# Norm of batch 0's FFN output moved into the last FFN, operands kept in DRAM; 57 instead of 51 FFN units in batch 1's first pass

## What is computed

```
x = x + layernorm(attn(layernorm(x)))     # projections, conv, heads' coefficients,
                                          # a recurrence over the 2048 tokens, group norm, gate, out_W
x = x + layernorm(ffn(layernorm(x)))      # router: mean over tokens -> 2 of 8 experts, softmax weights
# ffn: y_k = gelu(x @ W1[k] + b1[k]) @ W2[k] + b2[k];  out = w_0 y_0 + w_1 y_1   (k: the two chosen experts)
```

## Time and profile before

| | |
|---|---|
| median of 3 runs | 1680.47 us (1678.22 to 1681.45) |
| profiled execution | 1677.81 us, span 1675.6 us |
| TensorE matmul busy | 1248.9 us (75%) |
| VectorE busy | 1267.0 us (76%) |
| ScalarE busy | 409.7 us (24%) |
| GpSimd busy | 68.0 us (4%) |
| mean granted clock of TensorE | 0.879 |
| DMA | 94.34 MB, 56 GB/s over the span |

### The profile page before, as it was taken

One profiled execution on the slowest core, in us unless ns is written; L12 is line 12 of the kernel. 1 busy time (PEld: TensorE's weight loads), 2 busy tenths in 40 slices (PEclk: granted clock), 3 DMA queues, 4 the chain that ended last, 5 costly groups with the idle time before them and its releaser, 6 DMA issues. The chain is left out here.

```text
span 1675.6 us, 12210 instructions
## 1 busy us (share of the span) xinstructions
PE 1248.9 (75%) x4124; PEld 736.0 (44%) x4124; DVE 1267.0 (76%) x1885; ACT 409.7 (24%) x628; POOL 68.0 (4%) x32
## 2 busy tenths in 40 slices
PE   3970554513688888589699999396888786899997
PEld 1440222202344445345465555263544454566665
DVE  4769999998999985758789999987999957100111
ACT  2431000000002015343532232132010143323332
POOL 0000012110000000000001211100000000000000
PEclk9995767656799999779899999698999997999999
DMA  4000100003011120210023222214111010222221
GB/s 151 1 7 0 50 38 38 38 0 126 13 50 38 38 100 6 104 54 7 26 76 101 88 88 76 75 39 176 50 38 39 11 51 1 82 76 78 73 76 75
DMA packets 51676, 94.34 MB, mean 56 GB/s; under 512 B 4640, under 2 KB 39840, under 8 KB 50720
## 3 DMA queue, kind: packets, MB, share of 16 engines
q1 hardware_dynamic: 51616, 93.58, 16.0%
HBM read 73.64 MB, written 19.92 MB: 56 GB/s over the span
## 5 line engine op out<-in xcount | busy, mean ns | idle before, releaser
L486 PE MATMUL ps<-wshare,uT 128*128 128x512 f32 x512 | 244.3, 633 | 55.7 <-DVE kz L1261 55.7
L593 PE MATMUL ps<-kz 128*128 128x256 f32 x1024 | 245.2, 383 | 20.0 <-ACT kz L786 15.4
L579 PE MATMUL ps<-kz 128*128 128x512 f32 x512 | 243.3, 598 | 3.5 <-DMA kz<-in_w 3.3
L593 PEld LDWEIGHTS ps<-kz 128*128 128x128 f32 x1024 | 196.0, 192 | 103.6 <-issue 64.0
L486 PEld LDWEIGHTS ps<-wshare,uT 128*128 128x128 f32 x512 | 101.4, 204 | 178.8 <-issue 117.7
L428 PE MATMUL ps<-wshare,xnT 128*128 128x512 f32 x256 | 146.2, 724 | 35.2 <-ACT ps L661 35.2
L786 ACT ACTIVATE kz<-ps,small 128x512 f32<-128x512 f32 x128 | 87.4, 685 | 296.0 <-PE ps L579 295.8
L1419 DVE TENSOR_TENSOR kz<-ps,b_s 128x256 f32<-128x256 f32 x16 | 6.3, 413 | 180.7 <-PE ps L593 180.7
L579 PEld LDWEIGHTS ps<-kz 128*128 128x128 f32 x512 | 98.3, 193 | 80.6 <-issue 74.6
L420 PE MATMUL ps<-ident,uT 128*128 128x128 f32 x256 | 44.0, 302 | 113.4 <-DVE work L1139 79.1
L721 ACT ACTIVATE kz<-ps 128x512 f32<-128x512 f32 x32 | 19.1, 597 | 371.4 <-PE ps L471 371.4
(11 more groups left out here) (250 smaller groups left out, 1793.4 us busy)
## 6 DMA issues: line engine op xcount, KB each, us to landing
kz<-in_w SPq DMA_DIRECT2D x128, 256.0 KB, 2.9
kap_d<-kz SPq DMA_DIRECT2D x26, 512.0 KB, 2.7
kz<-kap_d SPq DMA_DIRECT2D x26, 512.0 KB, 3.2
uT<-in_x SPq DMA_DIRECT2D x8, 512.0 KB, 5.9
wshare<-in_wq SPq DMA_DIRECT2D x2, 2048.0 KB, 7.8
kz<-in_x SPq DMA_DIRECT2D x2, 2048.0 KB, 12.9
coef<-in_x SPq DMA_DIRECT2D x2, 2048.0 KB, 7.7
wshare<-in_wk SPq DMA_DIRECT2D x2, 1024.0 KB, 11.1
```

The source lines that it names most:

```text
L486: t = mm(ps[:, 2 * (j % 2) + c, :], uT3[:, k, j * P:(j + 1) * P], wq_s[:, k, c, :], start=(k == 0), stop=(k == KI - 1))
L579: t = mm(ps[:, 4 + i % 2, :], w1_r[r][:, k, (f % 2) * P:(f % 2 + 1) * P], x2T[:, k, n * 512:(n + 1) * 512], start=(k == 0), stop=(k == KM ...
L593: t = mm(ps[:, 6 + q // 2, (q % 2) * DM:(q % 2 + 1) * DM], hbuf(i)[:, q * P:(q + 1) * P], w2_r[r][:, f % 2, :], start=(f == 0 and q % 2 == ...
```

## The change

`expert_norm` is gone. After batch 0's FFN its output is stored in DRAM (`f_d`), and the combined bias too (`b2_d`, one row); VectorE does only the two bias instructions (`output_bias`) between `chunk_scan` and `pass_2`. In the last FFN SyncE loads f, bias and x1 into `uT` and `xnT`, which are free then, and `first_norm` does batch 0's norm on VectorE ahead of batch 1's first block; the scaling is on VectorE instead of ScalarE. ScalarE's square root for it (`first_root`) stands behind unit 8. The output of batch 0 is stored behind weight pair 13. In `UNITS` the last entry is 57, so that six of the 13 units behind `turn_ends` lie in the last step of pass 1. The kernel's work is otherwise the same.

```diff
-UNITS = [15] + [15 + 12 * i // 5 for i in range(L)]
+UNITS = [15] + [15 + 12 * i // 5 for i in range(L - 1)] + [57]
...
+        f_d = nc.dram_tensor("f_d", (P, L, DM), F32).ap()
+        b2_d = nc.dram_tensor("b2_d", (1, DM), F32).ap()
...
-        x1_back = kz[:, 5120:9216].rearrange("p (j d) -> p j d", j=L)
...
+        f_back, x1_back, b2_back = x_in, x_c, xnT[:, 0, 0:DM]
...
                 if b > 0:
                     load_pairs(b - 1, chosen, pairs_for(UNITS[L]), NF // 2)
-                    sp.wait_ge(h_ready, b * NF)
-                    sp.wait_ge(x1_stored, 16 * b)
-                    sp.dma_start(x1_back, x1_d[:]).then_inc(x1_loaded, 16)
-                    sp.wait_ge(d_done, b * NF)
+                    sp.wait_ge(b2_ready, b)
+                    sp.dma_start(b2_d[:], b2_s[0:1, 0]).then_inc(b2_stored, 16)
+                    sp.wait_ge(f_used, b * NCH)
+                    sp.dma_start(f_d[:], r_tok).then_inc(f_stored, 16)
                 for j in range(3, L):
                     if b > 0 and j == 5:
-                        sp.wait_ge(out_ready, b)
-                        sp.dma_start(out[b - 1].rearrange("(c j) d -> c j d", j=L), x1_back).then_inc(out_stored, 16)
+                        sp.wait_ge(f_stored, 16 * b)
...
-            load_pairs(B - 1, chosen, 0, NF // 2)
+            load_pairs(B - 1, chosen, 0, WR)
+            sp.wait_ge(f_stored, 16)
+            sp.dma_start(f_back, f_d[:]).then_inc(f_loaded, 16)
+            sp.wait_ge(b2_stored, 16)
+            sp.dma_start(b2_back, b2_d.to_broadcast([P, DM])).then_inc(b2_loaded, 16)
+            sp.wait_ge(x1_stored, 16)
+            sp.dma_start(x1_back, x1_d[:]).then_inc(x1_loaded, 16)
+            load_pairs(B - 1, chosen, WR, 14)
+            sp.wait_ge(out_ready, 1)
+            sp.dma_start(out[0].rearrange("(c j) d -> c j d", j=L), x1_back).then_inc(out_stored, 16)
+            load_pairs(B - 1, chosen, 14, NF // 2)
...
                 if b > 0:
                     experts(b - 1, UNITS[L], NF)
-                    last_root(b - 1)
-                    act.wait_ge(out_stored, 16 * b)
...
+                    if i == 8 and b == B - 1:
+                        first_root()
                     if f == 3 and n > 0 and b == B - 1:
                         block_root(n - 1)
...
-            def last_root(b):
-                act.wait_ge(fin_vec, b + 1)
+            def first_root():
+                act.wait_ge(fin_vec, 1)
                 af(t1, mv[:, :, 1], ACT.Sqrt, bias=eps5).then_inc(fin_act, 1)
-                act.wait_ge(fin_ln, b + 1)
-                for j in range(L):
-                    af(r_tok[:, j], r_tok[:, j], ACT.Identity, scale=rs2[:, j:j + 1], bias=nb[:, j:j + 1]
-                       ).then_inc(fn_ready, 1)
...
+            def first_norm():
+                dve.wait_ge(f_loaded, 16)
+                dve.wait_ge(b2_loaded, 16)
                 for j in range(L):
-                    dve.wait_ge(f_used, b * NCH + j // 4 + 1)
-                    t = mark(tt(r_tok[:, j], r_tok[:, j], b2c, ADD))
+                    t = mark(tt(f_back[:, j], f_back[:, j], b2_back, ADD))
                     if j > 0:
                         after(t - (2 if j > 1 else 1))
-                        stats(j - 1, r_tok[:, j - 1])
+                        stats(j - 1, f_back[:, j - 1])
                 after(t)
-                moments(stats(L - 1, r_tok[:, L - 1])).then_inc(fin_vec, 1)
+                moments(stats(L - 1, f_back[:, L - 1])).then_inc(fin_vec, 1)
+                dve.wait_ge(fin_vec, 1)
+                dve.wait_ge(fin_act, 1)
                 link(v.reciprocal(rs2, t1))
+                link(stt(nb, mv[:, :, 0], -1.0, rs2, MUL, MUL))
+                dve.wait_ge(x1_loaded, 16)
+                for j in range(L + 1):
+                    if j < L:
+                        t = mark(tsc(f_back[:, j], f_back[:, j], rs2[:, j:j + 1], nb[:, j:j + 1], MUL, ADD))
+                    if j > 0:
+                        after(t - 1 if j < L else t)
+                        a = tt(x1_back[:, j - 1], f_back[:, j - 1], x1_back[:, j - 1], ADD)
+                        if j < L:
+                            t = mark(a)
+                        else:
+                            a.then_inc(out_ready, 1)
+                dve.wait_ge(out_ready, 1)
...
                 chunk_scan(b)
                 if b > 0:
-                    expert_norm(b - 1)
+                    output_bias(b - 1).then_inc(b2_ready, 1)
                 pass_2(b)
```

More of the change, by code:

```diff
@@ L162, in build @@
         rn_ready = sem("rn_ready")
-        fin_ln = sem("fin_ln")
-        fn_ready = sem("fn_ready")
         x1_stored = sem("x1_stored")
         x1_loaded = sem("x1_loaded")
+        f_stored = sem("f_stored")
+        f_loaded = sem("f_loaded")
+        b2_ready = sem("b2_ready")
+        b2_stored = sem("b2_stored")
+        b2_loaded = sem("b2_loaded")
         k_ready = sem("k_ready")
@@ L1387, in choose @@
                 dve.wait_ge(pool_ready, b + 1)
+                if b > 0:
+                    dve.wait_ge(b2_stored, 16 * b)
                 link(v.tensor_reduce(psum1, ps[0:1, 5, 0:L], AX.X, ADD))
@@ L1410, in last_norm @@
                 b2c = b2_s[:, 0]
-                dve.wait_ge(eb_loaded, b * 64 + 64)
-                link(tsc(b2c, b2c, wbc[:, 0:1], None, MUL))
-                link(stt(b2c, b2_s[:, 1], wbc[:, 1:2], b2c, MUL, ADD))
+                first_norm()
+                link(output_bias(b))
                 for n in range(NCH):
@@ L1437, in last_norm, with output_bias @@
                             tt(x1_tok[:, j], r_tok[:, j], x1_tok[:, j], ADD).then_inc(out_ready, 1)
-            def expert_norm(b):
-                x1 = x1_back
+            def output_bias(b):
                 b2c = b2_s[:, 0]
@@ L1443, in expert_norm @@
                 link(tsc(b2c, b2c, wbc[:, 0:1], None, MUL))
-                link(stt(b2c, b2_s[:, 1], wbc[:, 1:2], b2c, MUL, ADD))
+                return stt(b2c, b2_s[:, 1], wbc[:, 1:2], b2c, MUL, ADD)
+            def first_norm():
+                dve.wait_ge(f_loaded, 16)
+                dve.wait_ge(b2_loaded, 16)
                 for j in range(L):
-                    dve.wait_ge(f_used, b * NCH + j // 4 + 1)
-                    t = mark(tt(r_tok[:, j], r_tok[:, j], b2c, ADD))
+                    t = mark(tt(f_back[:, j], f_back[:, j], b2_back, ADD))
                     if j > 0:
                         after(t - (2 if j > 1 else 1))
-                        stats(j - 1, r_tok[:, j - 1])
+                        stats(j - 1, f_back[:, j - 1])
                 after(t)
-                moments(stats(L - 1, r_tok[:, L - 1])).then_inc(fin_vec, 1)
-                dve.wait_ge(fin_vec, b + 1)
-                dve.wait_ge(fin_act, b + 1)
+                moments(stats(L - 1, f_back[:, L - 1])).then_inc(fin_vec, 1)
+                dve.wait_ge(fin_vec, 1)
+                dve.wait_ge(fin_act, 1)
                 link(v.reciprocal(rs2, t1))
[L1456 to L1462, removed]
+                link(stt(nb, mv[:, :, 0], -1.0, rs2, MUL, MUL))
[11 more added lines that the diff above has]
+                dve.wait_ge(out_ready, 1)
             link(v.memset(eps5, 1e-5))
```

## The result

The changed kernel has a median of 1657.49 us in 4 runs (1657.15 to 1658.23), the kernel before, measured beside it, 1679.35 us in 4 (1677.92 to 1681.45): ratio 0.9869, 95% interval 0.9852 to 0.9887. That is 21.9 us, against a forecast of 24.9. Two later measurements gave 1652.45 (one run, before 1680.72) and 1653.75 (five runs, before 1681.79; ratio 0.9847, 0.9827 to 0.9867), so 28 us. The profiled execution took 1658.23 us with a span of 1656.3, 19.3 less than the span before. To know how much of this is the change, one has to look at where in the span the time goes.

The account below looks back on a forecast made before the run. VectorE's norm was taken to end last before pass 2, TensorE's start states 4.3 us earlier. With both shortened, 24.9 us come off the 1680.47 us median, giving 1655.5 us, range 1651 to 1661.

Parts of the forecast that it names:

- (1): Last step of pass 1: six moved FFN units, 20.66 us, fit TensorE's hole with 1.8 us left; turning not delayed.
- (2): Between chunk scan and pass 2: batch 0's norm leaves VectorE's path, which is ready at about 1123.3 us instead.
- (3): Start of pass 2: VectorE waits 4.3 us for TensorE's start states, copies at about 1127.65 us; 24.9 us saved.
- (4): SyncE between the passes: new stores and loads and the later kappa reloads stay hidden, cost nothing.
- (5): Last FFN: loads, VectorE's norm and ScalarE's square root are hidden; 0 us charged for table changes, bounds 0 and 0.4.
- rival of the holding clock: Turning of the ends: TensorE's clock holds, 1.2 and 1.0 us more come off, 27.1 us saved, 1653.3 us; chance 0.10.
- the output's landing: Last FFN: batch 0's FFN output lands 7.9 to 14.1 us after its load's issue; 1452 us taken.
- scatter of the rest: Range of the total: runs spread 1.5 us each way, clock switching in later stages moves the end by 2.
- late-landing rivals: Last FFN: output landing at 26 us costs 6, 1661.5 us, chance 0.07; at 50 us, 1685.5 us, slower, chance 0.03.

Follow-up runs that it names:

- e5: The changed kernel traced again with no edit; span 1650.6 us, copy of the start states 53.47 us behind the end of pass 1.
- e9: The changed kernel once more, no edit, timed beside the kernel before; median 1653.75 us in five runs, ratio 0.9847.
- e4: The changed kernel with the last entry of UNITS 59 instead of 57; median 1653.51 us in four runs, kernel before 1683.07.
- e12: The changed kernel with 58 units and 26 unused matmuls between the two turnings of the ends in batch 1; median 1652.87 us, ratio 0.9827.
- e3: The changed kernel with the last entry of UNITS 58 instead of 57; median 1653.08 us in four runs, kernel before 1683.07.
- e11: The changed kernel with 59 units again, timed beside the others; median 1653.50 us in five runs, ratio 0.9823 to the kernel before.

## Why the prediction was right

**Point by point.** (1) The six units fit the hole; 1.80 us are left, as forecast, at full clock, and the first turning is not late (6.74 us from the marker in both kernels). The last unit of batch 0 ends 44.0 us behind the marker, forecast 43.5. (2) VectorE is ready at the marker + 49.1. (3) The wait for the start states is 4.89 us (4.37 and 4.39 in e5 and e9), forecast 4.3, and the copy stands 54.03 us behind the marker (53.47 in e5 and e9), forecast 53.5. The 0.5 us of the first trace is the unit behind the second turning (3.55 us for four matmuls instead of 3.00): the clock rose a little later. (4) VectorE waits for no kappa load in pass 2; from the copy to the group norm it takes 193.78 us, 194.10 before. (5) The last FFN is as short with the norm as without it. Against the kernel before it is equal in e9 (224.7 us from the first unit's start to the last one's end) and 1.7 us shorter in the first two traces (223.0), since its first eight matmuls took 3.67 us there and 5.37 before; that is luck of the clock and no merit of the change.

The rival of the holding clock was rightly held unlikely: TensorE stood 5.49 us between the turnings and the second ran at the low level. Its mechanism is real, as e4 and e12 show. Against e3 the turning became shorter there by 1.3 us and the unit by 1.7, where it was priced with 1.2 and 1.0. Little of that reached the copy: in e4 the eighth unit and the slow turning of the start states used up all but 0.3 us, in e12 the filling and the scan's end all but 0.9.

**What was off.** Of the last FFN's estimates the one for the output's landing held: it landed 10.3 us after its issue, within the 7.9 to 14.1. But VectorE needs the bias too, which is issued behind it and landed 10.7 us after its own issue; that is what VectorE's first instruction waited for, 11.3 us behind the output's issue, where I had taken 12. x1 landed 15.3 us after its issue, beyond the 14.1 that I had as the slowest. VectorE's first instruction of the norm, then issue to landing by the DMA rows:

```profile
1433.57 0.81 DVE L1460 TENSOR_TENSOR uT<-uT,xnT 128x256 f32<-128x256 f32 x2 [16.18 <-DMA xnT<-b_d]
...
uT<-f_d SPq DMA_DIRECT2D x1, 2048.0 KB, 10.3
uT<-x_d SPq DMA_DIRECT2D x1, 2048.0 KB, 15.3
...
xnT<-b_d SPq DMA_DIRECT2D x1, 128.0 KB, 10.7
```

It cost nothing: x1 was there 15 us before VectorE added it, the variance was ready 6.3 us ahead of GELU 8's end, and VectorE waited 8.03 us for ScalarE's root and 14.77 us more for block 1. The term that was truly too small is the scatter of the rest. I gave 2 us for the clock in later stages and 1.5 for the runs, and nothing for the stages ahead of the change; marker positions from 1074.0 to 1080.4 for code that is the same so far make it 6 us. In the traces this is most of what lies between one measurement of the changed kernel and the next (spans 1656.3, 1650.6 and 1651.6; markers 1080.36, 1075.89 and 1074.96), and it is the likely reason why the measurements showed 22 us once and 28 twice. The profiled execution of before, on which the sum was built, had gone the early way. The change's own sum was right to 0.5 us. That the median came within 2.0 us of the forecast owes something to luck, since the same program gave 1657.49 and 1653.75 in two measurements, on either side of 1655.5; both lie in the range. The price of the late-landing rivals was too low by the clock: 5.8 us lost for a gap of 3.8.

## What to carry to other kernels

Where two engines' chains end close to each other ahead of a step, cost both up to that step and take the later; here the two edits are worth 8.5 and 4.3 us alone and 24.4 to 25.0 together, so testing either alone would have made the change look poor. Before judging a change by the span, compare the traces at a marker just ahead of the edit: the stages in front may have moved by themselves. And price a new wait of TensorE with the clock that it loses, not with its length alone.

## What the runs showed of the hardware

TensorE standing 1.8 us between two turnings kept its clock for a turning of twelve transposes (1.50 us with 59 units), standing 4.03 us it did not (2.79 us with 58), and standing 3.72 us ahead of the start states it did not either (1.97 us for eight, otherwise 1.04). Filling the 4 us with matmuls that nothing uses kept the clock (1.47 us). One program came to the same instruction between 1074.96 and 1080.36 us in three traces. The fourteen traces of this case fall into two groups 5 us apart in the stages ahead, where TensorE's clock falls in its waits and the same 32 products behind the same wait of 6.13 us take 8.6 or 10.1 us. The chunk scan, which is VectorE's, repeats to 0.1 us: it ends 48.17 to 48.23 us behind the marker, but for e11 (48.10) and e12 (48.49), whose second turning was moved.
